# Where the unfolded blocks stand in a step: RAW_SPAN 0.92 to 0.58

## The reference

```python
def step(h, _):
    agg = jax.ops.segment_sum(h[s] * wn[:, None], d, num_segments=n)
    return ((1.0 - ALPHA) * agg + ALPHA * feat_0, None)
h, _ = jax.lax.scan(step, feat, None, length=K)      # K = 10, self loops in s, d
...
x = _layernorm(x + _L0_gnn_ref(x, edge_weight, src, dst), axis=-1)
x = _layernorm(x + _L1_gnn_ref(x, edge_attr_64, edge_index, ...), axis=-1)
```

## Time and profile before

| | us |
|---|---|
| median of 3 runs (9450.83 to 9453.82) | 9453.74 |
| the profiled execution | 9473.4 |
| its span | 9471.6 |

### The profile page before, as it was taken

The page is one execution under the profiler, slowest core; times in us unless marked ns, Lnnn a source line. Parts: engine busy times, 40 slices in busy tenths (PEclk is TensorE's granted clock), DMA queues, the critical chain, the costliest instruction groups (busy, mean ns, idle before and its releaser), DMA issues.

```text
span 9471.6 us, 147001 instructions
## 1 busy us (share of the span) xinstructions
PE 7991.6 (84%) x50439; PEld 4249.0 (45%) x50439; DVE 4547.1 (48%) x13980; ACT 5555.0 (59%) x7289; POOL 6999.3 (74%) x7533
## 2 busy tenths in 40 slices
PE   3877718999999999999999999999999766666666
PEld 3776613333333333333333333333333456666665
DVE  8999722333333333333333333333333555566666
ACT  1444306888787887888878788888888311111111
POOL 6777766777777777777777777777777577777776
PEclk5555558999999999999999999999999677777676
DMA  9993427999999999999999999999999555555554
GB/s 361 359 344 135 150 34 277 358 341 350 344 339 345 330 350 343 339 347 331 352 343 340 345 334 348 345 339 345 334 346 340 146 145 144 146 145 144 144 144 122
DMA packets 1397619, 2644.37 MB, mean 279 GB/s; under 512 B 684219, under 2 KB 723166, under 8 KB 1396609
## 3 DMA queue, kind: packets, MB, share of 16 engines
q1 hardware_dynamic: 989312, 2214.41, 65.5%
q0 software_dynamic: 233888, 257.77, 10.4%
q10 hardware_dynamic: 173664, 162.70, 5.4%
HBM read 2401.68 MB, written 232.39 MB: 278 GB/s over the span
## 4 chain that ended last, share of the span: by engine, by line
POOL 53%; issue 18%; PE 17%; DVE 8%; DMA 3%; ACT 1%; SPq 0%; DVEq 0%; POOLq 0%; ACTq 0%
POOL arena L1786 35%; POOL arena L1802 16%; PE banks L2635 12%; DVE arena L2125 4%; DVE arena L2196 2%; POOL dense L1755 2%; PE banks L2593 2%; DMA arena<-node_rows,src_idx 1%; ACT arena L1837 1%; PE banks L2697 1%; DVE arena L2215 1%; DMA arena<-dense 1%; DMA dense<-arena 1%; PE banks L2734 0%; DMA x_sb<-key_rows 0%
## 5 line engine op out<-in xcount | busy, mean ns | idle before, releaser
L1857 ACT ACTIVATE arena<-arena 128x1024 f32<-128x1024 f32 x4900 | 4762.6, 1044 | 1319.2 <-DMA arena<-dense 1261.2
L1786 POOL DMA_INDIRECT arena<-node_rows,src_idx x4528 | 4282.4, 946 | 1402.1 <-issue 1373.8
L2635 PE MATMUL banks<-arena,u_sb 128*64 128x512 f32 x11760 | 2610.9, 595 | 213.6 <-ACT arena L1857 213.5
L2635 PE MATMUL banks<-arena 128*64 128x512 f32 x12000 | 2673.1, 596 | 0.4 <-ACT arena L1857 0.4
L1802 POOL DMA_INDIRECT arena<-kv_rows,src_idx x1563 | 1485.6, 950 | 546.7 <-issue 476.3
L2635 PEld LDWEIGHTS banks<-arena,u_sb 128*64 128x64 f32 x11760 | 855.9, 138 | 1648.3 <-issue 1567.1
L2635 PEld LDWEIGHTS banks<-arena 128*64 128x64 f32 x12000 | 879.6, 138 | 1466.2 <-issue 1385.3
L1755 POOL DMA_INDIRECT dense<-arena x1028 | 1015.6, 988 | 401.4 <-issue 328.0
L2337 DVE TENSOR_SCALAR arena<-banks,step_rel,w_tab 128x64 f32<-128x64 f32 x4538 | 1213.8, 337 | 116.5 <-DVE arena L2348 87.6
L2409 DVE MEMSET arena<- 128x128 f32 x510 | 83.9, 165 | 2012.8 <-PE banks L2690 2009.0
L1939 ACT ACTIVATE banks<-arena 128x64 f32<-128x64 f32 x196 | 44.6, 228 | 1673.7 <-DVEq L2496 1673.7
(11 more groups left out here) (302 smaller groups left out, 5307.3 us busy)
## 6 DMA issues: line engine op xcount, KB each, us to landing
arena<-dense SPq DMA_DIRECT2D x3490, 512.0 KB
dense<-blank SPq DMA_DIRECT2D x8, 13056.0 KB, 110.6
arena<-in_dst_dram SPq DMA_DIRECT2D x195, 512.0 KB
arena<-node_rows,src_idx POOLq DMA_INDIRECT x4528
dense<-blank SPq DMA_DIRECT2D x1, 50000.0 KB, 218.1
arena<-in_edge_attr_dram SPq DMA_DIRECT2D x195, 256.0 KB, 3.2
x_sb<-key_rows ACTq DMA_DIRECT2D x27, 1792.0 KB
u_sb<-key_rows ACTq DMA_DIRECT2D x22, 1792.0 KB, 13.8
```

The costliest lines, as they stand in the source:

```text
L1786: gp.indirect_dma_start(out=rows_in[:, n % ROWS, s, :], out_offset=None, in_=rows, in_offset=bass.IndirectOffsetOnAxis(ap=idx.bitcast(U32) ...
L1857: nc.scalar.activation(planes[:, q % PLANES, half, :], ring[:, n % SLOTS, :], ACT.Relu, scale=-1.0 if half else 1.0).then_inc(planes_act, 1)
L2635: done = mm(banks[h * D:(h + 1) * D, sum_slot(k, g), :], u, rows[:, h * 512:(h + 1) * 512], start=first, stop=last, tile_position=(0, h * ...
```

## The change

One number of the table that sets the order:

```diff
@@ -46,7 +46,7 @@
 DENSE_LEAD = 5
 EARLY = 3
 LATE_FROM = 94
-RAW_SPAN = 0.92
+RAW_SPAN = 0.58
 AGG = 16 * P
 STREAMS = 4
```

## The result

The changed kernel takes 9491.72 us (median of 5 runs, 9483.41 to 9496.67), the kernel before, run beside it, 9450.83 (5 runs, 9443.07 to 9453.82). The ratio is 1.004, 95% interval 1.0029 to 1.0052: 41 us slower, where 36 were forecast. The number came out; most of the reasons did not.

The account below looks back on a forecast made before the run. GpSimd's gather issue was taken as the floor of steps 1 to 9, with DMA near its limit in the front. Terms +11 and +24 summed to +35 us: 9508 on the profiled execution, 9490 on the median; range 9438 to 9560.

Parts of the forecast that it names:

- The floor: Steps 1 to 9: GpSimd's issue of 471 gathers at 1.252 us sets the pace, 590 us a step.
- Measured 7.24 becomes 7.62 us per turn where DMA sets the pace: Front, step 0: 14 more loads over 52 turns slow each turn where the DMA engines are the bound.
- rival 1: Front: DMA has room and TensorE set the 7.24 us; +0 to +5 us, 9455, chance 0.24.
- The 0.38: Front: us added per turn by 0.141 MB more loads, taken from 0.39 at 359 GB/s.
- The +11 us of step 0: Step 0, turns 18 to 47: 29 turns x 0.38 us, passed whole to the border to step 1.
- The lag falls by 8.7 to 7.1: Back, turns 47 to 73: TensorE's delay after a turn's last gather shrinks from 15.8 us, against 4.4 at the end before.
- The +2.7 us per step: Borders between steps: reached 2.7 us later without cover, over 9 steps +24 us.
- rival 3: Borders: a full ring brings the load early and the eight 2.5 us waits vanish; -20 us, 9434, chance 0.09.
- the lead's 10 raw loads instead of 7: Step's first loads, before the border: argued against rival 3, as raw slots come free only when TensorE has used them.
- +24: Borders of steps: TensorE's remaining lag makes each 2.7 us later, 9 steps.
- the lag at turn 18 is still near 5: Step 3, front: sign that the forecast is wrong and DMA was no bound; 12 to 14 us forecast.
- Rival 2: Back: ScalarE, nearly full, cannot win anything back at 7.50 us per turn; +114 us, 9568, chance 0.17.

Follow-up runs that it names:

- the one with 0.30: Kernel before with group 0's raw blocks ending at 0.30 of the folded work, its first 8 left in place: 9527.39 us, ratio 1.0081.
- the kernel with the earlier store: Changed kernel with block 93's node store issued by ScalarE after the pairs of turn 76 instead of 77: 9440.28 us, ratio 0.9994.

## Why the prediction was right or wrong

**The floor.** That GpSimd's issue is the floor of steps 1 to 9 and that whatever makes a border later is paid in full was right: the waits and the times of the kernels above move together, and with no wait a step takes 588 to 589 us, forecast 590.

**The front.** "Measured 7.24 becomes 7.62 us per turn where DMA sets the pace" is the step that failed. It was 7.31, since DMA did not set the pace at 0.99 and 359 GB/s: it went on to 373 in this kernel and 386 in the one with 0.30. In step 0 a turn took 7.15 to 7.31 us at 312, 352, 359 and 373 GB/s alike, with TensorE recorded busy for all but 1.5 us of each stretch at most: that speaks for rival 1's reading, TensorE at its own pace, though no run made TensorE's work smaller. (The 0.38 itself was slightly off: 0.141 MB at 362 GB/s are 0.39 us.) Where the new front could be seen catching up, in the kernel with the earlier store, it was slower by some 0.08 us a turn. The +11 us of step 0 became 212 - 210 = 2 us; of that border's +6.7 about half, 3.6, comes with the lead alone (19.0 in place of 15.4 in the kernel where only it was changed), and 2.6 comes without it (18.0 in the kernel where only front and back were changed), each from one trace.

**The back.** "The lag falls by 8.7 to 7.1" was mis-sized at its start: there was next to no lag to fall, 6.6 us at turn 47 where 15.8 were forecast. The pace of the back, 7.17 forecast, was 187 / 26 = 7.19 in step 0. ScalarE had been costed rightly, 185.53 us busy.

**The border.** The +2.7 us per step were measured as +4.1, from a cause that was not in the sum. The prediction counted GpSimd's instructions and the stores as unmoved, and they are, as instructions. But a store waits behind what stands ahead of it on its queue. The prediction had both halves in hand, the chain with its 8.05 us load and, against rival 3, the lead's 10 raw loads instead of 7, and used them only to argue that nothing is gained there; it never priced two more loads at 1.6 us ahead of that store, +3.3, and 3.3 us later is where the last pair of the lead stood on the mean. The rest of the 4.1 are 0.6 us from the store's issue to the next gather and 0.2 us of the store's place. That the sum came out is luck: the forecast's +11 stood at the first border beside a measured +6.7 and its +24 at the others beside +33, most of it from a cause that it had not priced. It had the place of the cost right, the border.

**The signs it named.** Of what it said would prove it wrong, "the lag at turn 18 is still near 5" came true, helped by the later start of each step; the lags of 12 to 14, 14 to 18 and 6 to 9 us were 5.4, 6.6 and 3.2. The sum of waits (74.9, forecast 60 to 75), the share of 0.91 to 0.92 in the back and ScalarE full there came out as said. An agreeing total would have hidden this; the lag by turn did not.

**The rivals.** Rival 1's mechanism fits what was measured in the front; its time was wrong, since it too had no border. Rival 2 did not occur. Rival 3's end, the eight waits gone, is real but needs the store moved.

The Trainium skill's figure of about 358 GB/s per core (DMA: Bandwidth & Descriptors, "Where 436 GB/s comes from") was passed here for 162 us at 386 GB/s; its table's 425 for long loads on a core with an idle neighbour was not reached.

## What to carry to other kernels

When the order of work changes, look for what else stands on the same engine's list: a short DMA issue that another engine waits for inherits every wait of the instructions ahead of it. At a hand-over between iterations count the loads ahead of the last store that the next iteration needs, and price each at the pace of loads there; moving that store ahead of three pairs won more here, 12 us in the kernel before, than any tuning of the mix alone. A DMA share near 1 is not a ceiling: before a sum is built on it, load the queue more in one experiment.

## What the runs showed that was not expected

The share of the DMA engines went over 1 while the rate still rose: 359 GB/s at 0.99, 373 at 1.01 (both step 0, turns 18 to 47), 386 at 1.03 (step 3, turns 1 to 21, with more raw blocks). Moving one 32 KB store by one turn either way changed the kernel between 0.9986 and 1.0080 of its time. GpSimd's interval between gathers differed between the traces of kernels with the same list for it, 7.491 or 7.505 us per turn of six, 0.2% or some 10 us over the ten steps, which is as much as several of the effects looked for here; the waits at the borders are the surer measure.
